# A vision tower on one core: the low parts of expert 0 placed behind a wait, two steps of TensorE exchanged, the split of expert 1 moved

## The reference, cut to what matters

```python
h = tokens_of(x)                                  # layer norm of 3840 values, then a product with w
h = h + attn(layernorm(h))                        # 12 heads of 16; S = 64 tokens of an image
h = h + moe(layernorm(h))                         # 8 experts, the two largest of a router's softmax

def attn(x):
    q, k, v = split_heads(x @ qkv_w.T + qkv_b)
    s = q @ k.T * 16 ** -0.5
    allowed = (j % 8 == 0 and j <= i) or j == i or j == i - 1     # 8 strided keys, the token itself, its predecessor
    return softmax(where(allowed, s, -inf)) @ v @ out_w.T + out_b

def moe(x):
    for e in range(8):
        out += w_e * (gelu(x @ w1[e] + b1[e]) @ w2[e] + b2[e])    # 192 -> 768 -> 192
```

## Time and profile before

| | before |
|---|---|
| three timed runs | 200.71, 201.43 (median), 201.55 us |
| the profiled execution, its own time | 201.66 us |
| span from first to last instruction | 199.9 us |
| PE busy | 178.9 us, 89% of the span |
| PE weight loads | 154.3 us, 77% |
| DVE busy | 142.8 us, 71% |
| ACT busy | 115.4 us, 58% |
| POOL busy | 77.6 us, 39% |
| chain that ended last | PE 69%, DVE 11%, issue 6%, DMA 5%, ACT 3%, POOL 2% |

### The profile page before, as it was taken

One profiled execution on the slowest core, in us unless ns is written; L12 is line 12 of the kernel. 1 busy time (PEld: TensorE's weight loads), 2 busy tenths in 40 slices (PEclk: granted clock), 3 DMA queues, 4 the chain that ended last, 5 costly groups with the idle time before them and its releaser, 6 DMA issues.

```text
span 199.9 us, 3458 instructions
## 1 busy us (share of the span) xinstructions
PE 178.9 (89%) x1136; PEld 154.3 (77%) x1136; DVE 142.8 (71%) x319; ACT 115.4 (58%) x206; POOL 77.6 (39%) x102
## 2 busy tenths in 40 slices
PE   0599999985798987698999999999999999999994
PEld 0489749954566845577899999989989999989894
DVE  5487994498908638449976976878869869778753
ACT  2485753741221428456569579677596696785540
POOL 7873001125805051187034546266245344462000
PEclk9999999999859999999999999999999999999999
DMA  6999999100010177002700280450630810000002
GB/s 123 223 303 298 260 225 227 29 0 2 0 39 3 31 260 183 3 0 69 208 3 0 65 210 0 135 141 2 183 93 2 239 34 2 0 3 0 0 0 79
DMA packets 14691, 18.38 MB, mean 92 GB/s; under 512 B 2435, under 2 KB 10744, under 8 KB 14678
## 3 DMA queue, kind: packets, MB, share of 16 engines
q1 hardware_dynamic: 14134, 18.19, 34.3%
q10 hardware_dynamic: 544, 0.03, 0.2%
HBM read 17.44 MB, written 0.39 MB: 89 GB/s over the span
## 4 chain that ended last, share of the span: by engine, by line
PE 69%; DVE 11%; issue 6%; DMA 5%; ACT 3%; POOL 2%; SPq 2%; DVEq 0%; POOLq 0%; ACTq 0%
PE ps L371 30%; PE ps L1140 16%; PE ps L1142 7%; DMA early<-in_x 4%; DVE big_r L1215 3%; PE ps L826 2%; PE ps L1002 2%; PE ps L1184 1%; PE ps L1183 1%; DVE merge L1286 1%; PE ps L1182 1%; DVE norm L1393 1%; PE ps L939 1%; PE ps L828 1%; DMA shifted<-shifted 1%
## 5 line engine op out<-in xcount | busy, mean ns | idle before, releaser
L371 PE MATMUL ps<-big_r,wsplit 128*128 128x512 f32 (+1 forms) x255 | 62.8, 383 | 0.0
L1140 PE MATMUL ps<-wsplit,big_r 128*128 128x384 f32 x168 | 49.7, 355 | 0.7 <-DVE big_r L1215 0.7
L751 ACT ACTIVATE early<-ps,b1t 128x512 f32<-128x512 f32 x48 | 32.8, 683 | 29.8 <-PE ps L371 29.8
L1215 DVE TENSOR_TENSOR big_r<-early,big_r 128x512 fp32r<-128x512 f32 x48 | 38.4, 802 | 16.1 <-ACT big_r L333 15.6
L371 PEld LDWEIGHTS ps<-big_r,wsplit 128*128 128x128 f32 x255 | 43.1, 188 | 6.4
L1142 PE MATMUL ps<-wsplit,big_r 128*128 128x192 f32 x168 | 42.1, 250 | 0.0
L1140 PEld LDWEIGHTS ps<-wsplit,big_r 128*128 128x128 f32 x168 | 31.5, 188 | 3.0 <-DVE big_r L1215 0.9
L1142 PEld LDWEIGHTS ps<-wsplit,big_r 128*128 128x128 f32 x168 | 32.0, 190 | 1.3
L333 ACT ACTIVATE big_r<-early 128x512 fp32r<-128x512 f32 x48 | 30.3, 632 | 1.5
L1550 DVE SCALAR_TENSOR_TENSOR merge<-sq,gates,merge 128x192 f32<-128x192 f32 x32 | 26.9, 864 | 0.0
L1574 DVE SCALAR_TENSOR_TENSOR t_a<-ps,gates,merge 128x192 f32<-128x192 f32 x28 | 10.3, 412 | 6.3 <-PE ps L1142 6.3
(11 more groups left out here) (227 smaller groups left out, 290.3 us busy)
## 6 DMA issues: line engine op xcount, KB each, us to landing
stage<-in_L_ffn_w SPq DMA_DIRECT2D x4, 576.0 KB, 6.1
early<-in_L_ffn_w SPq DMA_DIRECT2D x4, 576.0 KB, 5.8
shifted<-in_L_tok_w SPq DMA_DIRECT2D x6, 288.0 KB, 9.6
early<-in_x SPq DMA_DIRECT2D x3, 512.0 KB, 7.0
stage<-in_L_ffn_w SPq DMA_DIRECT2D x4, 384.0 KB, 4.0
stage<-in_L_ffn_w SPq DMA_DIRECT2D x8, 192.0 KB, 4.9
early<-in_L_ffn_w SPq DMA_DIRECT2D x4, 384.0 KB, 3.2
early<-in_L_ffn_w SPq DMA_DIRECT2D x8, 192.0 KB, 3.8
```

Source lines behind the costliest of these rows:

```text
L371: mm = nc.tensor.matmul(dst, lhs, rhs, start=(first and n == 0), stop=(last and n == 4))
L751: nc.scalar.activation(gf[:, j % NG], ps[:, HPB[j % 4], :], ACT.Gelu, bias=b1t[:, bass.ds(k, 1)]).then_inc(s_gelu, 1)
L1140: nc.tensor.matmul(ps[:, AB[t], 0:2 * D], g_hi[:, j % NG, tok], w2c, start=(f == 0), stop=False)
L1215: return nc.vector.tensor_tensor(o, a, b, op)
```

## The change

Three edits. GpSimd waits for `s_nlo` to reach 2 ahead of the low parts of expert 0, that is until VectorE has made the low parts of `nt` for both groups. TensorE's `values(2)` and `values(3)` move ahead of `strided_scores(1)`, and `repeated_v(0)` and `repeated_v(1)` move from there to behind `near_by_heads(1)`. ScalarE's four copies for expert 1 move from behind the softmax into it, with the two waits they need, and `values(1)` moves ahead of `near_rows(1)`. No arithmetic is added or removed.

```diff
--- before.py
+++ after.py
@@ -550,6 +550,7 @@
                 if g == 0:
                     rstd(0, 0)
             rstd(0, 1)
+            pool.wait_ge(s_nlo, G)
             split_low_w1(pool, 0, 0)
             split_low_w2(pool, 0, 0)
 
@@ -720,26 +721,26 @@
             last_columns_again(0, 1, n1)
             high_parts(1, s_nt, NTB, nt, s_nhi)
             values(0)
+            act.wait_ge(s_emb, G)
+            act.wait_ge(d_stage[1], 16 * STAGE_DMAS)
+            split_high(1, 0)
+            split_high(1, 1)
             near_rows(0)
             transposed_q(1)
             exponentials(0)
+            values(1)
             near_rows(1)
             transposed_p(0)
-            values(1)
+            split_high(1, 2)
             exponentials(1)
+            split_high(1, 3)
             transposed_p(1)
-            act.wait_ge(s_emb, G)
-            act.wait_ge(d_stage[1], 16 * STAGE_DMAS)
-            split_high(1, 0)
             for g in range(G):
 
                 act.wait_ge(s_ao, g + 1)
                 copy(ao[:, 2 * g:2 * g + 2, D:], ao[:, 2 * g:2 * g + 2, P:D]).then_inc(s_aodup, 1)
                 high_parts(g, s_at, ATB, aot, s_ahi)
             nc.scalar.activation(table_in[:], neg_half[:, 0:1], ACT.Gelu)
-            split_high(1, 1)
-            split_high(1, 2)
-            split_high(1, 3)
             for g in range(G):
                 last_columns_again(1, g, n2)
                 high_parts(g, s_n2t, N2B, n2t, s_n2hi)
@@ -1089,13 +1090,13 @@
             transposed_q(1)
             near_scores(0)
             transposed_k(1)
+            values(2)
+            values(3)
+            strided_scores(1)
+            near_by_heads(1)
             repeated_v(0)
             repeated_v(1)
-            strided_scores(1)
-            near_by_heads(1)
             transposed_p(0)
-            values(2)
-            values(3)
             near_scores(1)
             strided_values(0)
             repeated_v(2)
```

## The result

The change makes the kernel faster: the median of four runs is 192.78 us (192.47 to 193.17) against 201.49 us before. The ratio is 0.9581, 95% interval 0.9544 to 0.9618. Some executions of a kernel are a few per cent longer at a lower granted clock: the ratios, as they stand on record, leave these out (here one of 205.25 us before), the medians don't. The profiled execution took 193.17 us, its span 191.5 us.

The account below looks back on a forecast made before the run. TensorE bounds the kernel from 38 us on, except in attention, where VectorE, GpSimd, ScalarE and a DMA take turns. Gains of 3.06 + 2.7 + 0.7 + 0.45 = 6.9 us take 201.43 to 194.5 us; range 193.2 to 196.8.

Parts of the forecast that it names:

- Edit 1, the hold: In attention, GpSimd's low parts hold VectorE's normalised(0, 1) at 3.73 us instead of 0.67; the wait removes 3.06 us.
- Rival C: normalised(0, 1) in attention is slow for a reason of its own, so only 1.15 us are gained: 200.3; chance 0.03.
- Edit 1, the clock: From values(0) to the keys of group 1, TensorE no longer runs at half clock after idling: 2.7 us gained.
- The low parts' new neighbours: GpSimd's low parts now run beside VectorE's scores(0), key_blocks(1) and near_products(1), fed from PSUM: no loss taken.
- Rival D: Low parts hold VectorE's PSUM-fed instructions in attention after all and the clock falls again: 2.05 us slower, 203.5; chance 0.03.
- Edit 2: Exchange on TensorE in attention: outputs(1) waits 1.3 us less, but residual(0) must wait for projection(0), so 0.7 us gained.
- Edit 3: ScalarE's moved copies for expert 1 end TensorE's wait at 80.37 for the copy for n2: 0.45 us gained, at most 1.0.
- Sum: All gains over the whole kernel: 3.06 + 2.7 + 0.7 + 0.45 = 6.9 us, giving 194.5 us.
- How the numbers follow: Step that set the whole kernel's range, 193.2 to 196.8 us, and the chances: forecast 0.70, faster 0.94.
- Rival A: In outputs(0), near_values(1) on GpSimd holds VectorE's second instruction, and 0.75 us of lateness reaches projection(0): 195.3; chance 0.13.
- Rival B: TensorE's clock falls all the same, in attention or a few microseconds later, so 2.7 us stay: 197.2; chance 0.11.
- the forecast's own sign: The prediction is wrong if the granted clock shows 0.50 in attention, or a VectorE row beside GpSimd exceeds its twin.

Follow-up runs that it names:

- the second profile: The whole change run once more without any edit, against the kernel before: median of six 192.76 us, ratio 0.9508; the profiled execution took 193.70 us.

## Why the prediction was wrong

Right about the hold and the clock, too small in its sum, wrong in one step of edit 2, and too narrow in what it let vary.

**Edit 1, the hold: right.** 3.06 us forecast, 3.06 measured. Rival C is out: the pair takes 0.67, 2.14 or 3.7 to 3.8 us with none, one or two GpSimd instructions beside it.

**Edit 1, the clock: right, 0.3 too small.** 2.7 forecast; 5.94 - 3.06 = 2.88 measured at the keys and 6.04 - 3.06 = 2.98 at scores(0), beyond my upper bound of 2.8; filling the idle time without touching the hold gives 2.87 at the keys (7.64 - 4.77). I had summed durations that overlap at their ends, and then taken the middle.

**The low parts' new neighbours: right.** The reduce of scores(0), for which no row existed, takes 0.41 us at 52.46 in the first profile beside POOL's second low part, and the products 1.64 us. Rival D is out.

**Edit 2: the step that failed.** The step is "0.7 us reach the path", because residual(0) must wait for projection(0). The cap itself is there: residual(0) waits 0.56 us for TensorE and no longer behind outputs(1), and bringing scores(1) forward changes nothing. The exchange brings residual(0) even less than forecast, 30.49 - 29.93 = 0.56 us, since low_parts(0) is 0.41 late and not 0.25 (27.63 against 27.22; scores(1) is 0.70 late behind scores(0), 0.8 forecast). But residual(0) isn't the only way to the end. outputs(1) comes 1.20 us sooner (30.02 - 28.82), and behind it on ScalarE come the high parts of group 1, the table for Gelu, the copies for expert 1 and the copy for `n2` that TensorE waits for. The load of the table starts 1.07 us sooner (32.06 - 30.99), and normalised(1, 1) and the end move with it: a wait alone without its later fall would end at 158.75 - 6.04 = 152.71 (an estimate from the profile of before), and with the exchange it is 151.64, so 1.07 us where 0.7 was forecast.

**Edit 3: right, 0.2 too small.** 0.45 forecast, 151.64 - 151.01 = 0.63 measured. Only 0.23 of it arises where the forecast had it, at the copy for `n2`. The other 0.40 are there at low_parts(0) already (27.63 - 27.23): moving the copies pays for the lateness that the exchange causes. The forecast had this as part of edit 2 and gave it too little: it kept 0.25 us of lateness at low_parts(0), and with all three edits there is none (27.23 against 27.22).

**Sum.** 3.06 + 2.98 + 1.07 + 0.63 = 7.74 us against 6.9 forecast: 0.8 of the error. In the forecast's own sum, 201.43 - 7.74 = 193.7, inside my range, as the like execution of 193.70 us is. What puts the median outside is the other 1 us (8.71 - 7.74), in the step "How the numbers follow": I took all that lies ahead of attention as one constant. It isn't. less_mean(0) starts anywhere from 37.06 to 38.69 us in the fourteen profiles, with no edit to tell them apart (once at 39.66, behind a low clock at 25 to 34 us), and the profiled execution of before was a late one. The timed runs have no profile, so that their starts make up this 1 us is argued from the profiles and not shown. A range of 3.6 us for the edits should have had this on both sides, and the median of 192.78 us would have been inside.

**Rival A, the hold in outputs(0): a near tie, and it cost nothing.** VectorE's multiplication started 0.11 us ahead of GpSimd (62.69 against 62.80), and the loser was GpSimd: 2.00 us for the pair, 1.70 before. In the kernel with the denominators moved GpSimd was first and VectorE lost 0.23 us, far from the 1.7 of the rival; GpSimd's first instruction kept its 0.87 us, and its second ended 0.3 us late in turn. The Trainium skill, page "SBUF — State Buffer", section "Who interferes with whom", has it that the first to issue keeps the pair of ports that VectorE and GpSimd share. The trace agrees in both orders: the multiplication keeps its 0.56 us when it is first, GpSimd its 0.87.

**Rival B, the clock falls all the same: not there, but elsewhere.** In the first profile of the change it falls at 65 us and costs 0.92 us (the end lies 151.93 against 151.01 behind less_mean). It is the one run of ten whose mean clock isn't 1.00. By the forecast's own sign, 0.50 in the clock's row in attention, that execution speaks against it and the second profile for it. With the wait alone every run had a fall. I had priced this at nothing, since the profile of before shows no fall behind 60 us.

**What the edits are worth one by one** is then not what they are worth together. Alone, the exchange and the copies measure as nothing (1.0019 and 1.0042). Behind the wait they bring 195.72 to 192.78, 2.9 us, of which 1.7 are their own (from scores(0) to the end it is 137.31 before and 135.61 after), 0.9 are the fall in the profile with the wait alone, which no longer comes (138.20 - 137.31), and the rest is how executions differ. With the wait but not the exchange ten of twelve runs have a mean clock of 0.991 or less, with both it is three of 24 (without the kernel with matmuls ahead of the first transposes, whose clock falls early). That the exchange is the cause of this is argued from these counts; no run takes it apart.

## What to carry to other kernels

When one VectorE instruction takes several times what its twin takes, look at what GpSimd runs beside it. Here each tensor_scalar of the norm, SBUF to SBUF, stood for one GpSimd instruction, some 1.5 us each; a pair of low parts with both inputs in SBUF took 2.5 us more than alone; and those fed from PSUM lost nothing. When one engine's wait is the cap on a gain, ask whether a second engine's queue carries the gain past it. Price TensorE's idle time twice, once as waiting and once as the slower clock behind it, and measure an edit on top of the one that cures the clock, since alone it may be swallowed by it. Before a range is given, ask how far apart two executions of the same kernel start the stage in question.

## What was not expected of the hardware

- The granted clock fell to 0.50 at 65 to 68 us in stretches in which TensorE is shown busy for the whole of 2 us, behind matmuls of one row or of half the array's width. The same matmuls stand in a profile without a fall, so the reason is open.
- The third group of eight transposes, at 11 us, takes 1.09 us in five profiles and 1.88 to 1.97 in eight (the one with matmuls ahead of them set aside), with the record of the granted clock at 1.00 both times. So that record doesn't tell them apart. The five start less_mean at 37.06 to 37.53 us, seven of the eight at 38.15 to 39.66, and one at 37.10. So the start that the forecast took as constant goes mostly with these transposes; that they cause it isn't shown.
- In the experiments the kernel before had mean clocks from 1.00 to 0.949 and times from 196.9 to 206.7 us; with the change the mean clock was 1.00 in nine of ten runs and the times lay within 1.5 us (192.22 to 193.70). A good part of what the change does is to take this chance away.
